# One copy for the fc2 weights, and the b2 load and its two preparations moved to the start

## The reference, cut to what matters

```python
q = (hidden_states @ Wq.T).astype(bfloat16); k = (hidden_states @ Wk.T).astype(bfloat16)
q, k = _apply_rope(q, pos, ROPE_BASE), _apply_rope(k, pos, ROPE_BASE)
scores = einsum('bqhd,bkhd->bhqk', q, k) / HDIM ** 0.5
exp_qk = where(causal, exp(scores), 0.0)
o = relu(exp_qk.sum(axis=-1) @ fc1_w.T + fc1_b)
attn = o @ fc2_w.T + fc2_b
...
h = relu(x @ W1[1] + b1[1])
y = h @ W2[1] + b2[1]
...
x = x + _layernorm(attn(_layernorm(x)))
x = x + _layernorm(ffn(_layernorm(x)))
```

## Time and profile before

| | |
|---|---|
| median of 3 runs | 93.06 us (91.72, 93.06, 93.29) |
| profiled execution | 91.72 us, its span 90.0 us |
| TensorE matmul, weight load | 92%, 55% of the span |
| VectorE, ScalarE, GpSimd | 85%, 79%, 63% of the span |
| granted TensorE clock | 0.997 |
| DMA | 7.64 MB, mean 85 GB/s |

### The profile page before, as it was taken

How to read it: one execution, slowest core, us unless ns; L and a number is a source line. 1 busy time by engine, 2 the same in 40 slices (tenths; PEclk the granted TensorE clock), 3 DMA queues, 4 the chain that set the end, 5 groups by cost and what they waited for, 6 DMA issues and landing times.

```text
span 90.0 us, 1535 instructions
## 1 busy us (share of the span) xinstructions
PE 82.5 (92%) x444; PEld 49.5 (55%) x444; DVE 76.6 (85%) x202; ACT 71.0 (79%) x210; POOL 56.8 (63%) x83
## 2 busy tenths in 40 slices
PE   4949999989999899979999999999999999999940
PEld 1317656354553444425544449696477975599830
DVE  2377999989999999899998799987999675997971
ACT  5017898999999999999999997899962569843840
POOL 6379576440910985699935445375748996897590
PEclk9999999999999999999999999999999999999998
DMA  0889996803624050220000000000120040005683
GB/s 26 244 240 277 312 294 170 205 15 87 149 63 123 0 117 0 60 60 0 0 0 7 0 0 0 0 0 0 53 64 11 0 120 0 0 25 149 179 246 101
DMA packets 11900, 7.64 MB, mean 85 GB/s; under 512 B 867, under 2 KB 10996, under 8 KB 11892
## 3 DMA queue, kind: packets, MB, share of 16 engines
q1 hardware_dynamic: 11892, 7.55, 31.7%
HBM read 3.61 MB, written 2.10 MB: 63 GB/s over the span
## 4 chain that ended last, share of the span: by engine, by line
PE 67%; ACT 20%; DMA 4%; POOL 2%; SPq 2%; issue 1%; POOLq 1%; DVE 0%
PE psum L735 24%; ACT psum L569 15%; PE psum L810 15%; PE psum L761 12%; PE psum L727 7%; DMA wqk_f<-wqk_t 4%; PE psum L789 3%; POOL rstd L505 2%; SPq L331 2%; PE psum L781 1%; ACT qk L521 1%; PE psum L710 1%; PE psum L765 1%; PE psum L772 1%; PE psum L800 1%
## 5 line engine op out<-in xcount | busy, mean ns | idle before, releaser
L505 POOL TENSOR_TENSOR rstd<-ve,half_neg 128x4 f32<-128x4 f32 (+2 forms) x38 | 34.8, 925 | 13.8 <-DVE ve L357 9.6
L569 ACT ACTIVATE psum<-psum 128x1024 f32<-128x1024 f32 (+7 forms) x48 | 36.7, 764 | 1.4 <-PE psum L761 0.6
L761 PE MATMUL psum<-qk_r 128*128 128x512 bf16 (+3 forms) x80 | 20.7, 349 | 1.4 <-ACT psum L569 0.6
L810 PEld LDWEIGHTS psum<-w_c,hid 128*128 128x128 f32 x128 | 15.6, 192 | 1.3 <-DVE cols_n L521 0.4
L735 PE MATMUL psum<-cols_n,wqk 128*128 128x512 f32 (+1 forms) x36 | 16.1, 556 | 0.0
L810 PE MATMUL psum<-w_c,hid 128*128 128x128 f32 x128 | 16.1, 278 | 0.0
L735 PE MATMUL psum<-cols_n,w_c 128*128 128x512 f32 (+1 forms) x36 | 15.6, 552 | 0.0
L761 PEld LDWEIGHTS psum<-qk_r 128*128 128x128 bf16 x80 | 6.6, 97 | 12.9 <-ACT psum L569 6.4
L727 PE MATMUL psum<-ident,rows_n 128*128 128x128 f32 x64 | 10.2, 277 | 0.1
L357 POOL TENSOR_SCALAR ve<-stats 128x4 f32<-128x4 f32 (+2 forms) x9 | 2.1, 233 | 11.6 <-DVE stats L642 6.6
L727 PEld LDWEIGHTS psum<-ident,rows_n 128*128 128x128 f32 x64 | 7.2, 141 | 3.8 <-issue 1.6
(11 more groups left out here) (85 smaller groups left out, 129.5 us busy)
## 6 DMA issues: line engine op xcount, KB each, us to landing
x_s<-x SPq DMA_DIRECT2D x7, 256.0 KB, 4.0
qk_swap<-qk SPq DMA_DIRECT2D x14, 128.0 KB, 2.3
out<-x_s SPq DMA_DIRECT2D x7, 256.0 KB, 2.3
table<-tables SPq DMA_DIRECT2D x3, 256.0 KB, 4.3
x_s<-x SPq DMA_DIRECT2D x2, 128.0 KB, 3.1
w_f<-w SPq DMA_DIRECT2D x2, 128.0 KB, 3.2
table<-tables SPq DMA_DIRECT2D x2, 128.0 KB, 4.3
out<-x_s SPq DMA_DIRECT2D x4, 64.0 KB, 1.6
```

The source lines that it names most:

```text
L505: ready[k].done(eng.tensor_tensor(rstd[:, g, STAT_SLOT[k], t], ve[:, g, STAT_SLOT[k], t], half_neg[:, 0:tiles], ALU.pow), n)
L569: exps.done(eng.activation(area, area, ACT.Exp, scale=scale_qk, accum_out=sums[:, g, s, j:j + 1]), n, j, s)
L761: mm = eng.matmul(psum[:, own[0] + i, 0:width], query, qk_r[:, g0 + c, 1, 0:width], start=True, stop=c < gb)
L810: mm = eng.matmul(bank[:, j * P:(j + 1) * P], hid[:, g, h, (j0 + j) * P:(j0 + j + 1) * P], w2_c[:, h, :], start=not seeded and h == 0, sto ...
```

## The change

Three things change. The load of b2 moves in STEPS from behind the tables to between load_x.6 and load_x.2. The steps b2mean and b2 on ScalarE move from behind w2 to ahead of +fc and to between the copies +tr1.3 and +tr1.4. And load_fc issues one DMA for the 17 rows of fc2 and its bias, where it issued one for 16 rows and one for the last; the fc matmul waits for 32 instead of 48. Of the table the piece below shows its first two lines; the rest of it differs by line breaks and the words named.

```diff
--- before.py
+++ after.py
@@ STEPS
-eps1.3.P load_x.6 eps1.0.D stat1.4 rstd1.0 wqk.0#0 load_x.2 rstd1.3 eps1.4.A norm1.0.D load_x.8 tr1.0#1 fc.0#2
+eps1.3.P load_x.6 eps1.0.D stat1.4 rstd1.0 load_b2.0 wqk.0#0 load_x.2 rstd1.3 eps1.4.A norm1.0.D load_x.8 tr1.0#1
...
@@ -311,8 +311,7 @@
             elif name == "load_fc":
-                eng.dma_start(fc_f[0:INNER, 2:2 + P], fc2_wb[0:INNER, :]).then_inc(l_fc, 16)
-                eng.dma_start(fc_f[INNER:ROWS, 2:2 + P], fc2_wb[INNER:ROWS, :]).then_inc(l_fc, 16)
+                eng.dma_start(fc_f[:, 2:2 + P], fc2_wb).then_inc(l_fc, 16)
                 eng.dma_start(fc_f[:, 0:2], fc1_wb).then_inc(l_fc, 16)
@@ -712,7 +711,7 @@
                     eng.wait_ge(s_repeat, 2)
-                    eng.wait_ge(l_fc, 48)
+                    eng.wait_ge(l_fc, 32)
                     bank = bank_of(name, n)
```

More of the change, by code:

```diff
@@ L39 @@
 load_x.3 blank.9#7 blank.1.256#7 load_x.0 repeat.0 load_x.4 mask.0 load_wqk.0 load_fc.0 stat1.3 load_x.1 stat1.0
[L40 to L46, removed]
+eps1.3.P load_x.6 eps1.0.D stat1.4 rstd1.0 load_b2.0 wqk.0#0 load_x.2 rstd1.3 eps1.4.A norm1.0.D load_x.8 tr1.0#1
+fc.0#2 +wqk.0.A rstd1.4 load_w2.0 stat1.1 +tr1.0.A norm1.3.D eps1.1.A load_x.5 fcmean.0 k.0#1 rstd1.1 norm1.4.D
+b2mean.0 tr1.3#0 load_x.7 +fc.0 q.0#3 norm1.1.D +tr1.3.A load_table.1 fcspread.0 stat1.6 tr1.4#2 b2.0 tr1.1#4
+load_table.4 stat1.2 +tr1.4.A q.3#0 load_b1.0 +tr1.1.A stat1.8 +k.0.A k.3#2 w2mean.0 load_table.0 eps1.6.D stat1.5
+rstd1.6 +q.3.A k.1#1 load_table.2 stat1.7 eps1.8.A k.4#4 +k.3.A rstd1.8 norm1.6.D +q.0.A swap.3 q.4#0 eps1.2.A +k.4.A
+rstd1.2 norm1.8.D tr1.6#3 +q.4.A load_table.3 cos.3.D rot.0#4 tr1.8#2 +tr1.6.A swap.4 norm1.2.D q.1#0 +tr1.8.A q.6#3
+cos.4.D eps1.5.A w2.0 sin.3.D tr1.2#2 +k.1.A rstd1.5 k.6#5 rope.3.D +q.6.A +tr1.2.A cos.0.D scores.2.2.0#3 eps1.7.A
 sin.0.D scores.2.3.0#1 exp.2.2.0 k.8#2 rstd1.7 sin.4.D exp.2.3.0 scores.2.0.0#3 rope.0.D scores.2.1.0#4 +k.6.A q.8#6
```

## The result

The changed kernel took 92.77 us in the median of 21 runs, the kernel before 91.86 us in as many runs beside it: the ratio is 1.0102, 95% interval 1.0084 to 1.012. That is 0.9 us slower, clear of noise, where 0.1 us faster was forecast. The profiled execution took 92.41 us, its span 90.7 us, where before it were 91.72 and 90.0. Each ratio is against the kernel before on the same chip.

What follows compares the result with a forecast made beforehand. The chain of waits, on TensorE, then early on ScalarE with two b2 steps, was taken as the bound. Terms -0.3 +0.05 +0.05 +0.1 gave -0.1 us: median 93.0 us from 93.06, range 91.3 to 94.0 (chance 0.89).

Steps and rivals of the forecast that it cites:

- part 3: Whether b2's data are there when ScalarE's moved b2 mean needs them; a cost of 0.05 us was taken.
- L: Time at which the moved b2 load lands: between 8.3 and 9.0 us, 8.5 taken.
- S: Shift of ScalarE's copy at 9.90 us, L-8.45 for L over 8.45: 0.05 us taken, bounds 0 and 0.55.
- part 4: One fc copy instead of two and b2 ahead of other loads, at the start: a cost of 0.1 us.
- part 1: Two b2 instructions leave ScalarE's chain at 16.71 us, ahead of the first scores: gain 0.3 us, bounds 0 to 0.4.
- Rival A: b2 lands late and ScalarE stalls at the b2 mean ahead of the fc2 subtraction: 93.2 to 93.8 us, chance 0.18.
- slack at x.7: Load x.7's statistics near 12.4 us have 0.3 us of slack, so a delay of 0.2 us is hidden.
- the 0.1 us for a busy engine: If all 17 fc rows lie on one DMA engine, later loads are up to 0.4 us later; 0.1 taken.
- Part 2, the gaps: The b2 steps go into ScalarE's waits for transposes before its copies at 9.04 and 9.90: cost 0 to 0.05 us.
- b2's own 4.4 us to landing: b2's time from issue to landing in its old place, used with x.6's 3.7 us to bound its new landing.

Runs made afterwards that it cites:

- e2: The changed kernel with the two fc copies of the kernel before restored; 1.010 of the kernel before.
- e3: The kernel before with only the b2 load moved behind load_x.6, ScalarE's b2 steps left at 16.7 us; 1.015 of before.
- e4: The changed kernel with b2's row laid out 128 times in memory, so 128 different rows are read; 0.9966 of the kernel before.
- e7: The changed kernel with b2's row laid out 16 times, each read for 8 neighbouring partitions; 1.0002 of the kernel before, 0.999 at the higher clock alone.
- e14: The changed kernel with b2's row laid out 8 times, each read by 16 partitions lying 8 apart; 1.0027 of before, 0.998 at the higher clock alone.
- e10: The changed kernel with the one-row b2 copy issued twice in a row, the second into an unread spare tile; 1.0327 of the kernel before.
- e1: The kernel before with only the two fc2 copies made one of 17 rows; 1.0004 of the kernel before.
- e11: The kernel of e4 with ScalarE's two b2 steps back at their old place behind w2; 1.0009 of the kernel before.
- e9: The kernel before without ScalarE's two b2 steps, the bias additions reading b2 as loaded; 0.9985 of the kernel before.
- e6: The kernel before with ScalarE's two b2 steps moved to 36 us, no DMA touched; 1.0073 of the kernel before, 1.004 at the higher clock alone.
- e12: The kernel before with ScalarE's b2 steps at 54 us, GpSimd's and VectorE's b2 steps behind them; 1.0027 of before, 1.001 at the higher clock alone.
- e13: The kernel of e12 with the b2 load also late, behind the load of w1 at 26.5 us; 0.9966 of the kernel before.
- e8: The kernel of e6 with the b2 load also late, behind the load of w1 at 26.5 us; 1.0039 of before, 1.003 at the higher clock alone.
- e5: The kernel before with b2's row laid out 128 times in memory and nothing moved; 0.9986 of the kernel before.

## Why the prediction was wrong

The step that failed is in part 3: the landing of b2, L = 8.5, and with it the term S, which the sum has at 0.05 us with bounds 0 and 0.55. "64 KB at the 340 GB/s of the full stretch are 0.2 us" helped to choose it, and the same 0.2 us is part 4's price for each load behind. So the copy was priced by its bytes. L was 9.6, and the old 9.90 copy came at 10.97: S was 1.07 us, and 0.92 where TensorE's block began. The copy took 1.8 us in which the engines moved 120 GB/s; at 300 GB/s these bytes take 0.7, so the copy's place cost 1.1 us of stream. x.2 landed at 10.6 instead of 8.9, and x.7 at 13.6 instead of 12.1. e2 and e3 show that the load does this, e4, e7 and e14 that it is the single row, and e10 that a second copy adds more still. Against the sum's -0.1 us the span shows 0.9 (b2 late), 0.2 (late loads) and -0.4 (part 1), together 0.7.

- Part 3, L: 8.5 was taken, 9.0 was the upper bound, and 9.6 was measured. Rival A had place and price nearly right (L = 9.6, a loss of 0.75, measured 0.7 in the span and 0.9 in the time), with a chance of 0.18; but its reason was saturation, and e3 shows that the loss is there without its stall.
- Part 4, slack at x.7: 0.3 us were there, 1.5 us of delay came. "0.2 is hidden" was right for 0.2. That the one fc copy costs nothing was right (e1), and the 0.1 us for a busy engine was too much if anything. By the Trainium skill ("DMA: Bandwidth & Descriptors", section "Why a DMA increments its semaphore by 16 and not by 1") a copy of 17 rows goes over one engine; e1 doesn't show whether it does, only that it doesn't matter here.
- Part 2, the gaps: right. With data in time the two steps cost nothing there (rows of e4: the copies at 8.73 and 9.60).
- Part 1, 0.3 us: right, and rather 0.4, its upper end. The traces show it (0.96 us instead of 1.37 ahead of the first scores), also in the changed kernel, where it took 0.4 off the loss. The times agree but can't show it: e11 against e4 0.4, e3 against e2 0.5, e9 0.1, each within about 0.4.
- The trace held a possible sign. b2's own 4.4 us to landing for 64 KB, more than x.6's 3.7 for 256 KB, was used as a latency in a queue. With its row in memory 128, 16 or 8 times it landed after 3.5 to 3.6 us, as one row in the old place after 3.8 to 4.7 (e6, e12, e1, e9), so the sign is a weak one. The low rate behind the tables in the kernel before (152 and 131 GB/s from 13.5 to 14.5 us, after 274) proves nothing by itself: e13, whose b2 copy is not there, moved 111 GB/s in that stretch. e13 is 0.6% faster than e12 (0.4% at the higher clock alone), with intervals that overlap; e8 is not faster than e6 at that clock. So what taking the copy out of the start is worth in the kernel before stays open.

Two kernels beat both: e4 and e13, each at 0.9966. e13 needs no other layout: b2 is loaded behind the load of w1 at 26.5 us, and prepared in ScalarE's gap at 54 us.

## What to carry to other kernels

A copy that reads one short row for all partitions is not priced by its bytes: look at what the DMA engines move while it is in the stream, and put it where nobody's load is behind it, or give it several rows to read. A load that is moved ahead of others must be priced at those others first, and only then at its own user. A step on the chain of waits is worth what stands between it and the second gate, and when that gate is a DMA, take the landing's scatter for the lower bound. Work that is moved on a busy engine must be priced at its new place too: here 0.4 us gained at 17 us, and 0.7 lost at 36. And before two kernels are compared, see that their executions had the same clock.

## What the runs showed of the hardware

The b2 copy reads one 512-byte row 128 times. With it in the stream the 16 engines moved, from 7 to 8 us, 124 GB/s (changed kernel), 85 (e2), 143 (e3) and, two copies in a row, 44 (e10). In the same window they moved 320 without it (kernel before), 287 (e1), 264 (e4), 296 (e7) and 276 (e14). There is one exception: e11, with the copy of e4, moved 171, so a rate of about half comes without the one-row copy too. The share of busy time of the engines fell to 0.18 in e10, so they had mostly no packet at work there. In the changed kernel it was 0.59 from 6.2 to 8.0 us, against 1.03, while the rate fell further, to 120 of 300 GB/s.

TensorE's granted clock fell to 0.50, the lower of its levels, 1.2 GHz, in the traced executions of e3, e5 and e6: between 7.5 and 8.5 us, until 11 to 12 us. Ahead of that TensorE had been without work for 0.84 to 0.86 us, until 5.84 to 6.09, and then worked. The pause alone doesn't decide it: in the kernel before it was 1.20 us until 6.05, and the clock stayed full. In the kernel before an execution with the lower mean clock (0.97) costs 1.4 us. In the changed kernel it costs 0.3 (92.85 against 92.6 us in the mean of 11 and 29 executions), and in e3, whose profiled execution took 93.04 us where three at full clock took 92.83 to 93.13, nothing that shows: where loads are late anyway, half the clock for 3 us is mostly hidden.
